# A cross-attention and expert kernel on one core: units of the first maxima put among the picks of the keys, three value projections moved into the loop, group 0's terms moved to GpSimd

## What is computed

```python
x = x + xattn(layernorm(x), ctx, ctx)      # scores - max, softmax, clip at 1e-12, 2048 keys
x = x + attn(layernorm(x))                 # rotary, alibi, 128 keys
x = x + ffn(layernorm(x))                  # 16 experts, best 4 of each row, gelu
```

## Time and profile before

| | us |
|---|---|
| median of three runs | 219.44 (215.56, 219.44, 219.81) |
| profiled execution | 215.47 |
| its span, first to last instruction | 213.7 |
| TensorE busy | 190.7 (89%) |
| VectorE busy | 146.4 (69%) |
| ScalarE busy | 149.1 (70%) |
| GpSimd busy | 76.0 (36%) |
| first reduction of a unit (VectorE) | 23.64 |
| first scores of the loop (TensorE) | 39.57 |
| last tile's products end, experts begin | about 130 |

### The profile page before, as it was taken

The page is one execution under the profiler, slowest core; times in us unless marked ns, Lnnn a source line. Parts: engine busy times, 40 slices in busy tenths (PEclk is TensorE's granted clock), DMA queues, the critical chain, the costliest instruction groups (busy, mean ns, idle before and its releaser), DMA issues.

```text
span 213.7 us, 6350 instructions
## 1 busy us (share of the span) xinstructions
PE 190.7 (89%) x2551; PEld 131.4 (61%) x2551; DVE 146.4 (69%) x263; ACT 149.1 (70%) x331; POOL 76.0 (36%) x111
## 2 busy tenths in 40 slices
PE   4799899699999989979899999799889999999691
PEld 1345436355555545435454667697769998999681
DVE  5286499999999988988999846746983447212120
ACT  4677684589999988857798972977664645367760
POOL 6123689989889970110200001510000114090000
PEclk9999999999999999999999999999999999999999
DMA  6935332237347322257787712300000000000000
GB/s 115 303 123 216 115 94 92 90 100 272 104 112 200 106 88 83 95 164 213 213 325 231 232 38 77 123 2 0 3 0 3 0 0 15 0 2 3 0 0 25
DMA packets 8690, 21.26 MB, mean 100 GB/s; under 512 B 1664, under 2 KB 2784, under 8 KB 8656
## 3 DMA queue, kind: packets, MB, share of 16 engines
q1 hardware_dynamic: 7344, 19.47, 28.7%
q0 software_dynamic: 592, 0.74, 1.5%
q10 hardware_dynamic: 720, 0.59, 0.8%
HBM read 17.52 MB, written 3.28 MB: 97 GB/s over the span
## 4 chain that ended last, share of the span: by engine, by line
PE 67%; DVE 14%; ACT 8%; issue 3%; DMA 3%; POOL 2%; ACTq 1%; DVEq 0%
PE ps L1271 14%; PE ps L1520 12%; PE ps L1252 10%; PE ps L1553 9%; PE ps L1214 6%; DVE mx L597 5%; PE ps L1119 4%; DMA wks<-in_wk 3%; PE ps L1126 2%; ACT cT L1052 2%; PE ps L1138 2%; PE ps L1411 2%; POOL wr L495 1%; DVE sm L708 1%; ACT ex L1030 1%
## 5 line engine op out<-in xcount | busy, mean ns | idle before, releaser
L597 DVE TENSOR_REDUCE mx<-ps 128x2 f32<-128x1024 f32 x64 | 75.2, 1220 | 7.0 <-PE ps L1214 6.8
L1030 ACT ACTIVATE ex<-ps 128x512 f32<-128x512 f32 x128 | 69.5, 595 | 14.4 <-PE ps L1252 11.3
L1271 PE MATMUL ps<-ex,vau 128*9 128x128 f32 x1024 | 40.0, 274 | 0.5 <-ACT oS L1042 0.4
L1520 PE MATMUL ps<-xT,w1s 128*128 128x128 f32 x256 | 34.4, 278 | 1.5 <-ACT cT L1052 1.3
L1520 PEld LDWEIGHTS ps<-xT,w1s 128*128 128x128 f32 x256 | 31.1, 192 | 2.9 <-ACT cT L1052 2.1
L803 DVE SCALAR_TENSOR_TENSOR xs<-ps,wr,xs 128x128 f32<-128x128 f32 x32 | 11.2, 350 | 31.4 <-PE ps L1553 31.3
L1271 PEld LDWEIGHTS ps<-ex,vau 128*9 128x9 f32 x1024 | 22.0, 90 | 16.1 <-ACT ex L1030 11.7
L1052 ACT ACTIVATE ex<-ps,b1s 128x128 f32<-128x128 f32 x64 | 18.2, 371 | 12.9 <-PE ps L1520 12.7
L1252 PE MATMUL ps<-qst,kst 64*128 64x128 bf16 x512 | 25.5, 217 | 1.3 <-ACT ex L1030 0.9
L1214 PE MATMUL ps<-kst,qst 64*128 64x512 bf16 x128 | 25.1, 380 | 1.6 <-DVE mx L597 1.6
L1252 PEld LDWEIGHTS ps<-qst,kst 64*128 64x128 bf16 x512 | 16.0, 93 | 16.4 <-ACT ex L1030 11.2
(11 more groups left out here) (207 smaller groups left out, 251.7 us busy)
## 6 DMA issues: line engine op xcount, KB each, us to landing
kst<-parts_d SPq DMA_DIRECT2D x84, 64.0 KB
w1s<-in_w SPq DMA_DIRECT2D x8, 512.0 KB, 4.4
kst<-in_w SPq DMA_DIRECT2D x8, 512.0 KB, 4.6
parts_d<-w1s SPq DMA_DIRECT2D x4, 768.0 KB, 3.7
cT<-in_ctxT SPq DMA_DIRECT2D x3, 512.0 KB, 5.2
cT<-in_ctxT SPq DMA_DIRECT2D x2, 256.0 KB, 5.0
picks<-in_pick ACTq DMA_DIRECT2D x1, 384.0 KB, 5.4
qkvs<-in_qkvw POOLq DMA_DIRECT2D x1, 192.0 KB, 3.4
```

What stands on the lines that cost most here:

```text
L597: dve.tensor_reduce(out=mx2[:, b, 2 * pair:2 * pair + 2, f], in_=ps[:, bank:bank + 2, :], axis=AX.X, op=ALU.max).then_inc(s["redA"], 1)
L1030: act.activation(ex[:, e % NE, :], ps[:, EBANK["exp", e], :], ACT.Exp, scale=SCALE).then_inc(s["exp"], 1)
L1271: last = pe.matmul(ps[32 * j:32 * j + DK + 1, 7, 128 * hg:128 * hg + 128], vau[:, NK * b + c, GH * hg + j, :], ex[:, (2 * t + j % 2) % NE, ...
L1520: last = pe.matmul(ps[:, SELF[j % 2], 128 * n:128 * n + 128], w1s[:, f0:f0 + 128], xT[:, (b % B) * S:(b % B + 1) * S], start=True, stop=True)
```

## The change

Nothing that is computed changes. On TensorE units 0 and 1 move ahead of the last key pick, batch 1's keys go one unit later, values 2, 3 and 4 go behind unit 8, and values 5, 6, 7 into tiles 3, 11 and 19 of the loop, with a place each in the rotation of the three banks. The fillers go. VectorE no longer makes group 0's terms, GpSimd does; its other terms move against its own work. SP writes out batch 1's parts between the last stacks of batch 0. ScalarE follows TensorE's order.

```diff
+        VALS_AT = {3: 5, 11: 6, 19: 7}
...
+                if t in VALS_AT:
+                    out.append(("vals", VALS_AT[t]))
...
-        V_BANK = [2, 3, 2, 3, 5, 6, 4, 5]
+        V_BANK = [2, 3, 5, 7, 5]
...
                 stack(0, p)
-            parts_out(2)
-            parts_out(3)
+                if p >= PAIRS - 3 and p < PAIRS - 1:
+                    parts_out(p - PAIRS + 5)
...
             for n in range(NG, 2 * NG):
                 k_parts(n)
+                if n == NG:
+                    max_terms(0)
+            max_terms(1)
...
-                if c == 0:
-                    max_terms(1)
-                if c == 2:
+                if c == 1:
                     max_terms(2)
+            max_terms(3)
...
-                if src is tri_in:
-                    max_terms(3)
 
             ones(6, 8)
+            max_terms(4)
...
-            max_terms(4)
...
-                if u == 7:
-                    dve.wait_ge(s["mxd"], 1)
-                    dve.wait_ge(s["init"], 1)
-                    m = mpad[:, 0].rearrange("p r (a c) -> p (r a) c", a=2)
-                    link(dve.tensor_copy(m[:, :, 0], mx[:, b, hs]))
-                    link(dve.tensor_tensor(mxr[:], mx[:, b, hs], m[:, :, 0], ALU.subtract))
-                    link(dve.tensor_copy(m[:, :, 1], mxr[:]))
-                    dve.tensor_tensor(m[:, :, 2], mxr[:], m[:, :, 1], ALU.subtract).then_inc(s["mpad"], 1)
...
             rows(0)
+            v_piece(4, V_BANK[4])
             for t in range(TILES):
                 exps(t, 0)
                 exps(t, 1)
+                if t in VALS_AT:
+                    v_piece(VALS_AT[t], EBANK["vals", VALS_AT[t]])
...
-                    pe.wait_ge(s["va"], 4)
+                    pe.wait_ge(s["va"], 2)
...
                 if t == 0:
-                    pe.wait_ge(s["va"], 2 * NG)
+                    pe.wait_ge(s["ksq1"], NG)
+                    pe.wait_ge(s["va"], 5)
```

More of the change, by code:

```diff
@@ L983, in _ @@
             k_set(2)
-            v_piece(2, V_BANK[2])
+            q_set(1)
             k_set(3)
-            v_piece(3, V_BANK[3])
-            q_set(1)
             q_set(2)
@@ L990, in _ @@
                 k_plain(NG + n)
-            for n in range(NG, 2 * NG):
-                v_piece(n, V_BANK[n])
+            v_piece(2, V_BANK[2])
+            v_piece(3, V_BANK[3])
             def least():
@@ L1120, in keys, with vals @@
                     .then_inc(s["kproj"], 1)
-            def vals(n):
-                bank = V_BANK[n]
+            def vals(n, bank):
                 for j in range(4):
@@ L1183, in bank_free @@
                         pe.wait_ge(s["mrow"], i + 1)
+                    elif kind == "vals":
+                        pe.wait_ge(s["va"], i + 1)
                     elif kind == "sums":
@@ L1217, in unit @@
                 last.then_inc(s["unitA"], 1)
[L1219 to L1223, removed]
             def turn(g):
@@ L1229, in turn @@
                     pe.wait_ge(s["init"], 2)
-                    pe.wait_ge(s["va"], NG + 2)
+                    pe.wait_ge(s["ksq1"], 3)
                 bank_free(("turn", g))
@@ L1290, in _ @@
             pe.wait_ge(d_wv, 16)
-            vals(0)
+            vals(0, V_BANK[0])
             key_rows(1)
-            vals(1)
+            vals(1, V_BANK[1])
             key_rows(2)
-            pe.wait_ge(s["va"], 1)
-            vals(2)
+            unit(0)
+            query_rows(1)
+            unit(1)
             key_rows(3)
[L1298 to L1301, removed]
+            unit(2)
             query_rows(2)
-            unit(1)
-            pe.wait_ge(s["kset"], NG)
+            unit(3)
             keys(4)
-            unit(2)
+            unit(4)
             keys(5)
-            unit(3)
+            unit(5)
+            unit(6)
             pe.wait_ge(s["qset"], len(Q_ROUNDS))
             keys(6)
-            unit(4)
+            unit(7)
             pe.wait_ge(s["ksq1"], 1)
             keys(7)
-            unit(5)
+            unit(8)
             pe.wait_ge(s["ksq1"], 2)
[L1316 to L1325, removed]
+            vals(2, V_BANK[2])
             unit(9)
-            fill(3)
+            vals(3, V_BANK[3])
+            unit(10)
             turn(0)
-            fill(3)
-            unit(10)
-            fill(1)
+            pe.wait_ge(s["va"], 3)
+            vals(4, V_BANK[4])
             unit(11)
@@ L1500, in _ @@
                     small(SMALL_AT[t])
+                if t in VALS_AT:
+                    bank_free(("vals", VALS_AT[t]))
+                    vals(VALS_AT[t], EBANK["vals", VALS_AT[t]])
                 if t + 8 + LEAD < N_UNITS:
```

## The result

The changed kernel takes 213.83 us (median of four runs, 213.63 to 214.25). Its ratio to the kernel before is 0.9919, 95% interval 0.9893 to 0.9946: a gain of 0.8%, clear of noise and inside 2%. The span goes from 213.7 to 212.1 us. (Three of the twelve executions of the kernel before that were made beside the last experiments take 219 us where the others take 215.3 to 216.1; why stays open, and the 219.44 ahead of the prediction was therefore no level to count from.)

A forecast was written before the change was run, and what follows sets the result against it. TensorE, VectorE and ScalarE together were taken to bound the loop. Front -5.0, hole -0.63, insertions +3.45 and GpSimd +0.6 give -1.6 us, put on the 219.44 median: 217.8 us, range 213.6 to 220.0.

The forecast's parts named there:

- rival B: In the loop, the inserted value projections cost nothing, taken up by VectorE's saved 2 us and TensorE slack: 214.4 us; chance 0.12.
- The front: Ahead of the loop, reduction 0 and unit 8 start earlier, so the first scores start at 34.55, 5.0 us earlier.
- VectorE's hole: ScalarE's 0.63 us hole at 42.92 goes, as VectorE no longer makes group 0's terms and is not behind.
- Insertions: Values 5, 6 and 7 in tiles 3, 11 and 19 of the loop cost 1.15 us each, 3.45 in all.
- GpSimd: Its in-order queue makes the terms: no cost at turn 1, 0.6 us of the lead lost at turn 4.
- The sum: Whole span: -5.0 - 0.63 + 3.45 + 0.6 = -1.6 us on 213.7, thus 212.1.
- SP: Batch 1's stacks start near 50.1 instead of 54.99; no term for this in the sum.
- VectorE's terms: Ahead of the loop, VectorE no longer makes group 0's terms, 2.0 us from 35.0 to 36.95; no separate term.
- A: In the loop, each inserted value projection costs only ScalarE's copy, 0.58 us: 216.1 us; chance 0.14.
- C: Ahead of the loop, units 8 to 11 wait for the stacks, pair 2 landing 1.1 us later: 219.1 us; chance 0.13.
- D: GpSimd's queue from group 3's maximum to turn 4 takes 13.0 us, before 12.43; with no lead, 220.0 us; chance 0.08.
- E: TensorE's clock falls to 1.2 GHz between 28.7 and 36 us without the fillers: +4.4, 223.8 us; chance 0.03.

The follow-up runs named there:

- values 2 had gained: Changed kernel with value projection 2 moved ahead of unit 8, in the wait for pair 2's rows: span 212.3 us.
- the run behind it: Changed kernel with values 2 ahead of unit 8, group 4's terms ahead of GpSimd's memset, group 1's ahead of its last key split: span 211.4 us, ratio 0.9904.

## Why the prediction was right

The range, 213.6 to 220.0, held the measured 213.83, close to its lower end. What was right is the saving: 1.6 us on the span, forecast and measured. The number put on record, 217.8, was 4 us too high, since I took the saving from 219.44; from the profiled execution's own 215.47 it gives 213.9. By its number alone the result is nearer to rival B (214.4) than to my forecast; it is the trace, point by point, that speaks for the forecast:

- **The front.** Forecast: reduction 0 at 19.7, unit 8 at 29.2, first scores at 34.55. Measured: 19.67, 29.38, 34.54. The wait for pair 2's rows was read from the end of SP's queue, 2.5 us behind the last issue. Measured by the start of unit 8, the rows were usable some 2.8 us behind the issue of their sixth transfer at 26.6 (SP issues one every 0.73 us from 22.94), and 2.6 to 2.8 us in the other runs.
- **VectorE's hole.** Forecast 0.63, measured 0.62 (lead 5.03 to 5.65). The size was right; the reason was not, or not alone: it closes just as well with group 0's terms on VectorE.
- **Insertions.** Forecast 1.15 each, upper bound 1.2; measured 1.21, 1.21, 1.20. The step that was off is the added 0.2 for the longer projection. The nearest row, 2.12 for its tile, already had the overlap with the scores lost; its projection takes 0.91 us, the values' 1.16, so 0.25 had to be added, and I rounded the sum down as well (2.32 to 2.3). It cost 0.17 us in the sum. The projection of the kernel before:

```profile
97.67 0.91 PE L1393 MATMUL ps<-qkvs,xT 128*128 128x384 f32 x2
```

- **GpSimd.** Turn 1 covered (its terms forecast for 43.05, done at 42.74; the turn at 43.20, without a wait); turn 4 forecast to lose 0.6, measured 0.33, as GpSimd's chain from the maximum (63.33) to the turn (76.02) took 12.7 us instead of 13.0.
- **The sum.** Forecast lead at the end of the loop 1.6, measured 1.78; after the loop 0.2 was lost, so that the span came out at 1.6. The last agreement is partly luck: -0.17 for the insertions, +0.27 at turn 4 and +0.09 at tile 5 that I had not foreseen stand against each other, and so does the 0.2 behind the loop.
- **SP** bought nothing, as the sum had it. **VectorE's terms** were worth 0.5 to 0.7 us, within a total that was right: I had them inside the front and the hole.
- **The median** was wrong, and with it the forecast's own range of 217.3 to 219.1. That the wider range held is owed to its lower end, which I had set by the profiled execution.
- **Rivals.** A and B fell: each insertion cost its whole time on TensorE. C fell: unit 8 did wait for its rows, but only until 29.38, near the forecast and not 1.1 us behind it. D named the right place, and turn 4 did wait, but the lead was past the point where it decides. E did not happen here (clock 1.00 from 24 to 37 us), but my ground against it, one long wait that cost nothing, was bad, as the kernel before without fillers shows.

## What to carry to other kernels

Price a piece that you move at both places: the same projection cost 1.06 us in a row of its kind ahead of the loop, with what it added to another wait, and 1.21 between bfloat16 pieces inside the loop. When a front gets faster, look down the queue of the engine that nobody waits for yet (here GpSimd): it took 0.33 us of the change's lead, 0.53 of the 0.62 that values 2 had gained, and 0.97 of 1.05 in the run behind it. Before you move a step forward in such a queue, check that its input is ready there. Fillers could be removed here where real work took their place, and not where it did not; look at the granted clock of the run, not at the length of single waits. And when a run is slower than expected, find the tile at which the distance grows before you name the cause: of the 2.9 us without fillers a third had nothing to do with the clock.

## What was not expected of the hardware

Three waits of 0.73 to 0.84 us with a few matmuls between them (1.69 us of work in 4) were followed by nearly 7 us at 1.2 GHz, which cost 1.8 us, while one wait of 1.42 us between full stretches left the clock at 1.00. In executions of one order, the rows of pair 2 became usable at times 0.5 us apart (28.89 to 29.38), most of it because SP's queue had started at times 0.5 us apart (22.44 to 22.94). In one run of fourteen TensorE stopped for 0.61 us inside a group of products, for nothing that the profile shows.
